# A gated MLP's feature tiles: ten instead of eight computed with seven block products for eight, and the block sums divided between VectorE and GpSimd

## The chip, the cores and the metric

One core of a Trainium2 chip runs the whole program. The metric is device time in microseconds (us) for one execution. Engines are named as the profile names them: PE is TensorE (matrix products), DVE is VectorE, ACT is ScalarE, POOL is GpSimd, and SP is SyncE, which here only issues DMAs. Each engine runs its own list of instructions in order and waits on semaphores.

## The reference, cut to what matters

The input x has 8 batches of 512 rows of 512 features. It is normalised to `xn`. One branch (a state-space layer) gives `s`, the other (a block with attention, a small modulation and a gated MLP) gives `g`, and the output is `x + s * g`. The change touches the gated MLP alone:

```
h = _rmsnorm(residual, ln2_w)                     # residual = xn, 512 features per row
gate_pre = h @ W_in_base.T + mod * (h @ A) @ B    # W_in_base: 2048 x 512, B: 16 x 2048
gate = silu(gate_pre)
up = h @ W_up_base.T                              # W_up_base: 2048 x 512
mlp_out = gate * up @ W_down.T                    # W_down: 512 x 2048
g = silu(residual + mlp_out)
out = x + s * g
```

`mod` is the modulation from the attention.

## The kernel before

The program computes the state-space branch first, then the attention (to about 1440 us of the span), then the MLP. The MLP is what the change touches, and it has two halves.

**Numbers in three products.** Each fp32 operand is split into a high part and its remainder; a product of two matrices is then high*high, high*low and low*high, so three matmuls stand for one (`project3`, lines 72 to 74). A high part comes from a copy into fp32r, the low part from a subtraction.

**First half.** The 2048 features of the MLP are 16 tiles of 128. Tiles 0 to 7 are computed in the plain way, batch by batch: step q = 8b + f is tile f of batch b, 64 steps in all. A step is, on PE, a "column" (gate: 4 pieces of the contraction by 3 matmuls and one for the modulation, line 2229; up: 12 matmuls) into the banks `PS[q % 2]` and `PS[2 + q % 2]`, and later a "down" (12 matmuls, lines 2253 to 2255) that adds into `PS[4..7]`. Between them stands the "product": ACT takes silu of the gate (`SG`, line 2279), DVE multiplies it with the up part (line 2302), ACT makes the high part `GH` (line 2282), DVE the low part `GL` (line 2304). PE's order is column q, down q - 1, column q + 1, down q: the product of step q has until PE has done down q - 1 and column q + 1. Steps 0 to 3 (EARLY) are done inside the attention. At the end of a batch DVE adds the skip `XT` to the four banks (`M`, line 2319) and SP stores them (`m_scratch`); in between DVE scales the skips (line 2309, four times).

**Second half.** Tiles 8 to 15 are taken as 4 units of 2 tiles, and the batches as 4 pairs. For a unit and a pair, the weights are a 2 x 2 block matrix (2 tiles by 2 halves of the contraction) and so are the rows (2 halves of the contraction by 2 batches). Their product is made with 7 block products for 8, from sums of blocks, for gate and for up. Step v (16 of them, `second_tensor`) is 14 block products of 6 matmuls, 4 modulation matmuls (line 2541) and 48 down matmuls (lines 2612 to 2614), 136 in all; ACT, DVE and POOL put the block products together (`U`, `P`, `G`, `HH`), and DVE adds the result to `MP` in SBUF (line 2704). After every pair (v = 4, 8, 12) silu, scaling by s and the skip finish the pair's 8 row tiles while the next pair runs. `SW` (7 sums of weights, two buffers), `DW2` and `XB` (7 blocks of rows) are loaded from scratch in DRAM.

**The jobs in between.** The sums of blocks must lie in DRAM when the second half begins. 36 jobs make them during the first half, all by POOL, through two buffers `JOB0` and `JOB1`: 16 "rows" jobs (7 instructions: add high and low, four sums of 256 columns, a cast and a subtraction to split 1024 columns), 16 "weights" jobs (8 instructions, a half of the contraction each, up to 896 columns wide) and 4 "outward" jobs (splitting a 1024-column piece of the down weights). `ffn_order` writes the order by hand: from q = 8 on, in two of three steps, the load of the next job, the job, and the store of its result. SP takes all loads and stores in this one order and waits, before each, for what it needs: a load for the last store from its buffer, a store for POOL.

**Passing over.** `second_ahead` (on SP) waits for the stores of all jobs and for 56 of 64 up parts, then loads `XB` 0 to 2, `SW` and `DW2` of the first unit, eight `MP` tiles, and after the last step the rest.

The names in the change: `GU` holds the split weights of the plain tiles, `DW` those of the down product, `FH`/`FL` the rows of a batch, `sw_scratch`, `dw_scratch` and `xt_scratch` the results of the jobs.

Of the kernel before, what the change touches and what calls it, by code (L numbers as in the profile page):

```python
# [19 lines left out]
HF = FF // 2  # L20
# [12 lines left out]
def build(nc, x, WinT, convw, convb, WxT, Alog, dtb, outWT, Dp, ln1, ln2, WqT, WkT, Wv, Wo, Aw, Bw, WgT, WuT, WdT,  # L33
          ident, umask, arow, maskt, maskT, out):
    ctx = ExitStack()
    with ctx:
# [2003 lines left out]
        GU.append(sb(re_, "GU1", [128, 4, 4, 512], F32R))  # L2040
# [3 lines left out]
        JOB = [sb(re_, "JOB0", [128, 2048], F32R)]  # L2044
        M1 = [sb(re_, f"M1{i}", [128, DM]) for i in range(4)]
        JOB.append(sb(re_, "JOB1", [128, 2048], F32R))
        re_.close()

# [15 lines left out]
        MP = [sb(hs, f"MP{i}", [128, DM]) for i in range(4)]  # L2064
        STR = [sb(hs, f"STR{i}", [128, DM]) for i in range(4)]
        MP += [sb(hs, f"MP{i}", [128, DM]) for i in range(4, 8)]
# [6 lines left out]
        sw_d = nc.dram_tensor("sw_scratch", [4, 128, 2, 2, 7, 2, 128], F32R, kind="Internal").ap()  # L2073
        dw_d = nc.dram_tensor("dw_scratch", [4, 128, 2, 2, DM], F32R, kind="Internal").ap()
# [792 lines left out]
```

## Time and profile before

| | us |
|---|---|
| median of 3 runs | 2478.18 |
| lowest and highest of them | 2475.45, 2478.62 |
| the profiled execution, its own time | 2479.31 |
| span of that execution's trace | 2477.3 |
| PE busy | 2400.3 (97%) |
| DVE busy | 1498.7 (60%) |
| ACT busy | 1108.8 (45%) |
| POOL busy | 708.8 (29%) |

The trace counts from the first to the last instruction; 2.0 us of the profiled execution's own time lie outside it. Matmuls are pipelined, so that one is shown as busy for longer than the distance to the next one; what a stretch of matmuls costs is read from their starts. An instruction of DVE or POOL that is held up by something other than a semaphore is shown as a longer instruction, not as idle time. In the page's chain of work that ended last PE has 80% and DVE 7%.

### The profile page before, as it was taken

How to read it: one execution, taken by the hardware profiler on the slowest of the kernel's cores; microseconds unless marked ns; L12 is line 12 of the kernel's file. 1: busy time of each engine (PE TensorE's matmuls, PEld its weight loads, DVE VectorE, ACT ScalarE, POOL GpSimd, SP SyncE). 2: the span in 40 equal slices, each digit the busy share in tenths (PEclk: the TensorE clock that was granted, in tenths of full speed). 3: DMA queues.
4: the chain of work that ended last, by engine and by line, in shares of the span. 5: the costliest groups of instructions: out<-in, count | busy, mean ns of one | idle time of the engine just before them, and what ended most of it. 6: DMA issues, size and time to landing. Idle time of an engine off the chain costs nothing.

```text
span 2477.3 us, 37647 instructions
## 1 busy us (share of the span) xinstructions
PE 2400.3 (97%) x13847; PEld 1944.4 (78%) x13847; DVE 1498.7 (60%) x3000; ACT 1108.8 (45%) x1895; POOL 708.8 (29%) x674
## 2 busy tenths in 40 slices
PE   7999999999999899999999999999999999999998
PEld 5878878778888777777777678888888887787876
DVE  7857667667565588888988853223332345454546
ACT  6444544544444377777777641111111233332333
POOL 4000000000001244454453616664647002121212
PEclk9999999999999999999999899999999999999999
DMA  4000100000003577676666426655555945555461
GB/s 146 18 35 1 35 18 18 35 18 18 17 1 107 184 208 215 201 201 192 178 182 201 129 77 208 217 198 188 194 199 175 351 174 205 203 189 219 163 245 68
DMA packets 190747, 348.65 MB, mean 141 GB/s; under 512 B 19008, under 2 KB 89664, under 8 KB 181840
## 3 DMA queue, kind: packets, MB, share of 16 engines
q1 hardware_dynamic: 188064, 345.91, 42.6%
q8 instruction: 112, 1.84, 0.3%
q10 hardware_dynamic: 2496, 0.29, 0.1%
q14 instruction: 75, 0.61, 0.1%
HBM read 234.70 MB, written 111.15 MB: 140 GB/s over the span
## 4 chain that ended last, share of the span: by engine, by line
PE 80%; DVE 7%; issue 5%; DMA 4%; ACT 2%; POOL 2%; SPq 1%; DVEq 0%; ACTq 0%; POOLq 0%
PE PS L72 12%; PE PS L74 12%; PE PS L73 12%; PE PS L1748 3%; PE PS L813 2%; PE PS L812 2%; PE PS L814 2%; PE PS L2253 2%; PE PS L2254 2%; PE PS L2255 2%; PE PS L1706 2%; PE PS L1725 2%; PE PS L1707 2%; PE PS L1708 2%; PE PS L2612 2%
## 5 line engine op out<-in xcount | busy, mean ns | idle before, releaser
L1912 DVE CUSTOM_DVE_ANT_0 PS<-PS,MK 128x512 f32<-128x512 f32 (+3 forms) x512 | 244.4, 503 | 70.5 <-PE PS L1725 68.7
L1848 ACT ACTIVATE PF<-PS 128x512 f32<-128x512 f32 (+1 forms) x384 | 201.0, 528 | 90.5 <-PE PS L1752 60.0
L2302 DVE TENSOR_TENSOR SG<-SG,PS 128x512 f32<-128x512 f32 x60 | 41.3, 688 | 290.9 <-PE PS L74 289.7
L72 PE MATMUL PS<-XH,WH 128*128 128x512 f32 x504 | 208.8, 414 | 0.0
L74 PE MATMUL PS<-XH,WL 128*128 128x512 f32 x504 | 197.6, 392 | 0.0
L73 PE MATMUL PS<-XL,WH 128*128 128x512 f32 x504 | 196.8, 390 | 0.0
L74 PE MATMUL PS<-FH,GU 128*128 128x512 f32 x480 | 187.9, 391 | 0.0
L73 PE MATMUL PS<-FL,GU 128*128 128x512 f32 x480 | 187.5, 391 | 0.0
L72 PE MATMUL PS<-FH,GU 128*128 128x512 f32 x480 | 187.4, 390 | 0.0
L1725 PE MATMUL PS<-KS,QS 96*128 96x512 f32 (+3 forms) x512 | 172.4, 352 | 13.2 <-DVE MX L1912 13.1
L72 PE MATMUL PS<-XB,SW 128*128 128x512 f32 x448 | 175.5, 392 | 4.4 <-ACT P L2669 3.6
L1917 DVE TENSOR_TENSOR PL<-PF,PH 128x1024 f16<-128x1024 f32 (+1 forms) x128 | 175.4, 1370 | 4.1 <-ACT PH L1853 4.1
L74 PE MATMUL PS<-XB,SW 128*128 128x512 f32 x448 | 175.3, 391 | 0.0
L73 PE MATMUL PS<-XB,SW 128*128 128x512 f32 x448 | 175.0, 391 | 0.0
L1748 PE MATMUL PS<-QS,KS 97*128 97x512 f32 (+3 forms) x512 | 170.1, 374 | 0.0
L1089 DVE SCALAR_TENSOR_TENSOR XC<-PS,CW,XC 128x511 f32<-128x511 f32 (+2 forms) x192 | 143.6, 748 | 33.6 <-ACT XC L950 28.6
L1853 ACT CAST PH<-PF 128x1280 f16<-128x1280 f32 x128 | 161.2, 1260 | 4.1
L2012 POOL TENSOR_TENSOR PL<-PF,PH 128x256 f16<-128x256 f32 x112 | 91.8, 819 | 190.9 <-ACT PH L1853 190.6
L2279 ACT ACTIVATE SG<-PS 128x512 f32<-128x512 f32 x60 | 36.0, 601 | 243.4 <-PE PS L2229 243.3
L2764 POOL TENSOR_TENSOR U<-U,P 128x512 f32<-128x512 f32 x16 | 20.8, 1297 | 386.5 <-ACT P L2669 386.5
L657 POOL TENSOR_TENSOR RSTD<-VT,MHALF 128x4 f32<-128x4 f32 x8 | 8.1, 1012 | 417.9 <-DVE VT L576 417.9
L1725 PEld LDWEIGHTS PS<-KS,QS 96*128 96x128 f32 x512 | 100.6, 203 | 27.1 <-DVE MX L1912 22.1
(352 smaller groups left out, 6644.5 us busy)
## 6 DMA issues: line engine op xcount, KB each, us to landing
SW<-sw_scratch SPq DMA_DIRECT2D x10, 3584.0 KB, 12.3
qk_scratch<-QT SPq DMA_DIRECT2D x128, 256.0 KB, 4.7
QS<-qk_scratch SPq DMA_DIRECT2D x96, 256.0 KB, 4.0
KS<-qk_scratch SPq DMA_DIRECT2D x96, 256.0 KB, 4.0
xt_scratch<-JOB SPq DMA_DIRECT2D x32, 512.0 KB, 3.5
XB<-xt_scratch SPq DMA_DIRECT2D x16, 1024.0 KB, 6.3
sw_scratch<-JOB SPq DMA_DIRECT2D x32, 448.0 KB, 3.3
DW<-dw_scratch SPq DMA_DIRECT2D x10, 1024.0 KB, 5.0
```

The lines of the kernel that those rows point to most:

```text
L72: pe.matmul(o, lh(k), xh(k), start=open_ and k == 0, stop=False, skip_group_check=True)
L73: pe.matmul(o, lh(k), xl(k), start=False, stop=False, skip_group_check=True)
L74: last = pe.matmul(o, ll(k), xh(k), start=False, stop=close and k == nk - 1, skip_group_check=True)
L812: pe.matmul(PS[bank][:, :], YH[u][:, c], OH[:, d, :], start=d == 0, stop=False, skip_group_check=True)
L1089: dve.scalar_tensor_tensor(out=y[:, j:], in0=p[:, 0:S - j], scalar=CW[:, d, 3 - j:4 - j], in1=y[:, j:], op0=ALU.mult, op1=ALU.add).then_in ...
L1725: t = pe.matmul(PS[2 + a % 2][:, at:at + n], QS[0:96, h, 128 * how:n], KS[0:96, h, 0:n], start=how != 1, stop=True, skip_group_check=True)
L1748: t = pe.matmul(p[:, at:at + n], KS[0:97, h, 128 * J:128 * J + 128], QS[0:97, h, 128 * J:512], start=len(how) == 2 and at == 0, stop=len(h ...
L1848: act.activation(PE_[u][:, o:o + at], PS[4 + a % 2][:, 0:at], ACT.Exp, scale=SC).then_inc(a_ex, 1)
L1853: act.copy(PH[u][:, :], PE_[u][:, :]).then_inc(a_ph, 1)
L1912: dve.tensor_tensor_reduce(out=p, in0=p, in1=MK[:, 512 - n:512], scale=1.0, scalar=NEG, op0=ALU.add, op1=ALU.max, accum_out=MX[w % 2][:, j ...
L1917: dve.tensor_tensor(PL[u][:, 0:n], PE_[u][:, 0:n], PH[u][:, 0:n], ALU.subtract).then_inc(a_rm, 1)
L2012: pool.tensor_tensor(PL[u][:, 1024:1280], PE_[u][:, 1024:1280], PH[u][:, 1024:1280], ALU.subtract).then_inc(a_rp, 1)
```

## The change

There are now 5 units of 2 tiles in the second half (tiles 6 to 15) and 6 plain tiles (`FIRST = 6`), so the first half has 48 steps and the second 20. The constants in waits follow. The two plain tiles' weights are not split in the first half any more (the slices 6 and 7 of `ffn_order`), and the skips are scaled at f = 4 instead of 6.

The jobs are laid out anew. The 16 rows jobs ("sums") are done by DVE, one in every second step from q = 8 to 38, behind that step's product and whatever else DVE has in it, through three buffers `JOBX`. POOL does 10 weights jobs, one in every fourth step, each now for the whole contraction (instructions twice as wide, up to 1792 columns) through a buffer `JOBW`, and 5 outward jobs through `JOBD`. SP has all of their loads and stores in one list.

In the second half, one modulation matmul goes to bank `DN[0]` instead of `ZG`; the first down product (t = 0) then waits for DVE's addition out of that bank, and t = 2 and 3 wait for earlier additions than before.

**DVE, first half, steps 6 to 9.** `SG` and `GL` are a step's product, `XT` the skips' scaling, `M` the end of a batch, `JOBX` a sums job. Before:

```order
L2302 TENSOR_TENSOR SG<-SG,PS 128x512
L2304 TENSOR_TENSOR GL<-SG,GH 128x512
L2309 TENSOR_SCALAR XT<-XT,MEAN,RSTD 128x512 x4
L2302 TENSOR_TENSOR SG<-SG,PS 128x512
L2304 TENSOR_TENSOR GL<-SG,GH 128x512
L2302 TENSOR_TENSOR SG<-SG,PS 128x512
L2304 TENSOR_TENSOR GL<-SG,GH 128x512
L2319 TENSOR_TENSOR M<-XT,PS 128x512 x4
```

The same engine in the changed kernel, the steps 9 and 10 with the job behind step 10:

```order
L2331 TENSOR_TENSOR SG<-SG,PS 128x512
L2333 TENSOR_TENSOR GL<-SG,GH 128x512
L2331 TENSOR_TENSOR SG<-SG,PS 128x512
L2333 TENSOR_TENSOR GL<-SG,GH 128x512
L2338 TENSOR_SCALAR XT<-XT,MEAN,RSTD 128x512 x4
L2420 TENSOR_TENSOR JOBX<-JOBX 128x1024
L2422 TENSOR_TENSOR JOBX<-JOBX 128x256
L2423 TENSOR_TENSOR JOBX<-JOBX 128x256
L2425 TENSOR_TENSOR JOBX<-JOBX 128x256
L2427 TENSOR_TENSOR JOBX<-JOBX 128x256
L2429 CAST JOBX<-JOBX 128x1024
L2431 TENSOR_TENSOR JOBX<-JOBX 128x1024
```

Seven instructions now stand between the product of an even step and that of the next.

**POOL, first half, its first work there.** Before, two rows jobs begin:

```order
L2385 TENSOR_TENSOR JOB<-JOB 128x1024
L2387 TENSOR_TENSOR JOB<-JOB 128x256
L2388 TENSOR_TENSOR JOB<-JOB 128x256
L2390 TENSOR_TENSOR JOB<-JOB 128x256
L2392 TENSOR_TENSOR JOB<-JOB 128x256
L2394 CAST JOB<-JOB 128x1024
L2396 TENSOR_TENSOR JOB<-JOB 128x1024
L2385 TENSOR_TENSOR JOB<-JOB 128x1024
```

Now a weights job (`JOBW`) and an outward job (`JOBD`):

```order
L2439 TENSOR_TENSOR JOBW<-JOBW,L2C 128x512
L2440 TENSOR_TENSOR JOBW<-JOBW,L2C 128x512
L2442 TENSOR_TENSOR JOBW<-JOBW 128x256
L2444 TENSOR_TENSOR JOBW<-JOBW 128x256
L2446 TENSOR_TENSOR JOBW<-JOBW 128x256
L2447 TENSOR_TENSOR JOBW<-JOBW 128x256
L2449 CAST JOBW<-JOBW 128x1792
L2451 TENSOR_TENSOR JOBW<-JOBW 128x1792
L2456 CAST JOBD<-JOBD 128x1024
L2458 TENSOR_TENSOR JOBD<-JOBD 128x1024
```

The rows jobs left POOL, and its longest instruction went from 1024 to 1792 columns.

**SP, the passage to the second half.** Before, the jobs' last stores and the loads of the second half:

```order
L2192 DMA XT<-in_x_dram 128x512 x4
L2355 DMA JOB<-in_WuT_dram 128x2x128 x2
L2374 DMA sw_scratch<-JOB 128x7x128
L2376 DMA sw_scratch<-JOB 128x7x128
L2359 DMA JOB<-in_WdT_dram 128x512 x2
L2374 DMA sw_scratch<-JOB 128x7x128
L2376 DMA sw_scratch<-JOB 128x7x128
L2374 DMA dw_scratch<-JOB 256x1x512
L2376 DMA dw_scratch<-JOB 256x1x512
L2449 DMA XB<-rh_scratch 128x1024
```

Now:

```order
L2381 DMA sw_scratch<-JOBW 128x1792 x2
L2235 DMA m_scratch<-M 128x512 x4
L2216 DMA XT<-in_x_dram 128x512 x4
L2374 DMA JOBW<-in_WuT_dram 128x512 x2
L2394 DMA dw_scratch<-JOBD 256x1x512 x2
L2381 DMA sw_scratch<-JOBW 128x1792 x2
L2490 DMA XB<-rh_scratch 128x1024
L2491 DMA XB<-rl_scratch 128x1024
L2494 DMA XB<-xt_scratch 128x2048 x2
L2477 DMA SW<-sw_scratch 128x7168
```

The load of the last weights job now stands behind the stores of a batch's four `M` tiles and the loads of the last skips.

The diff, cut to its core (the jobs' bodies keep their arithmetic):

```diff
-        PAIRS, UNITS = NB // 2, 4
+        PAIRS, UNITS, FIRST = NB // 2, 5, 6
...
+        WEIGHTS, OUTWARD, ROWS = 2 * UNITS, UNITS, 4 * PAIRS
...
-            yield "slice", 6
             yield "down", 3
-            ahead = 0
-            for q in range(EARLY + 1, 8 * NB):
-                b, f = divmod(q, 8)
+            for q in range(EARLY + 1, FIRST * NB):
+                b, f = divmod(q, FIRST)
...
-                if f == 6:
+                if f == FIRST - 2 or q == EARLY + 1:
                     yield "skips_scaled", b
-                if q == EARLY + 1:
-                    yield "slice", 7
-                if q >= 8 and q % 3 and ahead < len(jobs):
-                    if ahead == 0:
-                        yield "job", 0
-                    if ahead + 1 < len(jobs):
-                        yield "job", ahead + 1
-                    yield "job_kept", ahead
-                    ahead += 1
+                i = q - FIRST - 1
+                if i == -1:
+                    yield "weights_load", 0
+                    for n in range(3):
+                        yield "sums_load", n
+                if i < 0:
+                    continue
+                if i and i % 4 == 0 and i // 4 < WEIGHTS:
+                    yield "weights_load", i // 4
+                if i % 8 == 1 and i // 8 < OUTWARD:
+                    yield "outward_load", i // 8
+                if i >= 4 and i % 2 == 0 and i // 2 + 1 < ROWS:
+                    yield "sums_load", i // 2 + 1
+                if i % 4 == 0 and i // 4 < WEIGHTS:
+                    yield "weights_job", i // 4
+                if i % 8 == 2 and i // 8 < OUTWARD:
+                    yield "outward_job", i // 8
+                if i % 2 and i // 2 < ROWS:
+                    yield "sums_job", i // 2
+                if i % 4 == 2 and i // 4 < WEIGHTS:
+                    yield "weights_kept", i // 4
+                if i % 8 == 5 and i // 8 < OUTWARD:
+                    yield "outward_kept", i // 8
+                if i >= 3 and i % 2 and (i - 3) // 2 < ROWS:
+                    yield "sums_kept", (i - 3) // 2
...
-                sp.wait_ge(m_u, 60 if u == 0 else 8 * NB)
+                sp.wait_ge(m_u, FIRST * NB - 2 + 2 * u)
...
-            for r in range(2):
-                sp.wait_ge(j_st[r], j_st0[r] + 32 * len(range(r, len(jobs), 2)))
-            sp.wait_ge(m_u, 56)
+            sp.wait_ge(w_st, w_st0 + 32 * WEIGHTS)
+            sp.wait_ge(d_st, d_st0 + 32 * OUTWARD)
+            for r in range(3):
+                sp.wait_ge(x_st[r], x_st0[r] + 32 * len(range(r, ROWS, 3)))
+            sp.wait_ge(m_u, FIRST * NB - FIRST)
...
-                pe.wait_ge(n_ad, n_ad0 + 5 * v + 1)
-                modulate(pe, ZG, f1, b1, True).then_inc(n_pr, 1)
+                pe.wait_ge(*((n_ev, 8 * v - 3) if v else (m_fn, 4 * NB - 1)))
+                modulate(pe, DN[0], f1, b1, True).then_inc(n_pr, 1)
...
-                    if t < 2:
-                        pe.wait_ge(*((n_ev, 8 * v - 3 + t) if v else (m_fn, 4 * NB - 1 + t)))
+                    if t == 0:
+                        pe.wait_ge(n_ad, n_ad0 + 5 * v + 3)
+                    elif t == 1:
+                        pe.wait_ge(*((n_ev, 8 * v - 2) if v else (m_fn, 4 * NB)))
                     elif t < 4:
-                        pe.wait_ge(n_ad, n_ad0 + 5 * v + 5 - t)
+                        pe.wait_ge(n_ad, n_ad0 + 5 * v + t - 1)
...
-                dve.tensor_tensor(U3[0][:, :], U3[0][:, :], ZG[:, :], ALU.add).then_inc(n_ad, 1)
+                dve.tensor_tensor(U3[0][:, :], U3[0][:, :], DN[0][:, :], ALU.add).then_inc(n_ad, 1)
```

Here `m_u` counts up parts done, `n_ad` DVE's additions in the second half, `n_ev` the additions into `MP`.

## Rows read from the trace of the kernel before

**Rows 1.** The two largest waits of PE from 1440 us on: total, times, longest.

```profile
PE PS L2612 <- DVE HH L2743: 4.5, 3, 1.5
PE PS L72 <- ACT P L2669: 3.6, 3, 1.2
```

**Rows 2.** Busy time by stretch: PE, PEld, DVE, ACT, POOL, PE clock, DMA share, GB/s.

```profile
1500.00:1900.00 400.00, 400.00 (x1755) 329.60 (x1755) 129.26 (x142) 57.52 (x95) 245.47 (x230) 1.00 0.59 194
```

**Rows 3.** Timeline of DVE in two steps of the first half: start, duration.

```profile
1506.03 0.69 DVE L2302 TENSOR_TENSOR SG<-SG,PS 128x512 f32<-128x512 f32 x1 [6.38 <-PE PS L74]
1507.40 2.19 DVE L2304 TENSOR_TENSOR GL<-SG,GH 128x512 fp32r<-128x512 f32 x1 [0.69 <-ACT GH L2282]
...
1514.46 0.69 DVE L2302 TENSOR_TENSOR SG<-SG,PS 128x512 f32<-128x512 f32 x1 [4.88 <-PE PS L74]
1515.84 0.69 DVE L2304 TENSOR_TENSOR GL<-SG,GH 128x512 fp32r<-128x512 f32 x1 [0.69 <-ACT GH L2282]
```

**Rows 4.** Timeline of DVE in the second half: one instruction in two steps.

```profile
2031.97 0.69 DVE L2712 TENSOR_TENSOR G<-G,PS 128x512 f32<-128x512 f32 x1 [10.54 <-PE PS L74]
2062.98 0.69 DVE L2712 TENSOR_TENSOR G<-G,PS 128x512 f32<-128x512 f32 x1 [10.54 <-PE PS L74]
```

**Rows 5.** Timeline of POOL beside the first step of rows 3.

```profile
1506.64 2.40 POOL L2385 TENSOR_TENSOR JOB<-JOB 128x1024 f32<-128x1024 f32 x1 [62.85 <-DMA JOB<-rl_scratch]
1509.12 1.07 POOL L2387 TENSOR_TENSOR JOB<-JOB 128x256 f32<-128x256 f32 x1
```

**Rows 6.** Groups by line, first half: count, busy us, mean ns, idle before.

```profile
L2304 DVE TENSOR_TENSOR GL<-SG,GH 128x512 fp32r<-128x512 f32 x60 | 64.7, 1078 | 41.2 <-ACT GH L2282 41.2
```

**Rows 7.** Views of single DVE lines: duration ns min/median/max, first and last start.

```profile
L1205 DVE TENSOR_TENSOR EX<-EX,DTB x8: 1221/1224/1226, 63.6 to 754.0; 128x1024 f32<-128x1024 f32 x8
L1221 DVE TENSOR_TENSOR PFM<-MD,MASK x16: 418/422/426, 68.5 to 759.3; 128x256 f32<-128x256 f32 x16
L2309 DVE TENSOR_SCALAR XT<-XT,MEAN,RSTD x32: 534/831/2653, 1474.2 to 1948.3; 128x512 f32<-128x512 f32 x32
L2319 DVE TENSOR_TENSOR M<-XT,PS x32: 678/681/689, 1491.8 to 1960.5; 128x512 f32<-128x512 f32 x32
```

**Rows 8.** The same of POOL lines, by tile.

```profile
L1985 POOL TENSOR_TENSOR STGC<-STGC,L2C x8: 1034/1266/2286, 1365.4 to 1402.3; 128x512 f32<-128x512 f32 x8
L2387 POOL TENSOR_TENSOR JOB<-JOB x16: 736/744/1097, 1509.1 to 1868.9; 128x256 f32<-128x256 f32 x16
L2394 POOL CAST JOB<-JOB x16: 1039/1041/1406, 1512.5 to 1872.2; 128x1024 fp32r<-128x1024 f32 x16
L673 POOL TENSOR_TENSOR WL<-ZS,WH x1: 4694/4694/4694, 19.4 to 19.4; 128x2048 fp32r<-128x2048 f32 x1
```

**Rows 9.** DMA landing times: issues by line from 1500 to 1900, then `SW` at 1920 to 1930.

```profile
xt_scratch<-JOB SPq DMA_DIRECT2D x32, 512.0 KB, 3.5
JOB<-in_WdT_dram SPq DMA_DIRECT2D x6, 256.0 KB, 2.9
DMA to landing us min/median/max: 17.8/17.8/17.8
```

**Rows 10.** Timeline of SP and PE at the passage to the second half.

```profile
1925.70 0.58 SPq L2436 DMA_DIRECT2D SW<-sw_scratch  x1
...
1958.52 0.39 PE L72 MATMUL PS<-XB,SW 128*128 128x512 f32 x1
```

**Rows 11.** Timeline of PE and DVE: a plain step, then the pair's change (v = 4).

```profile
2038.70 0.68 DVE L2728 TENSOR_TENSOR U<-U,PS 128x512 f32<-128x512 f32 x1
2040.67 0.39 PE L2612 MATMUL PS<-DW,HH 128*128 128x512 f32 x1
2104.83 0.39 PE L2612 MATMUL PS<-DW,HH 128*128 128x512 f32 x1
2106.02 0.69 DVE L2728 TENSOR_TENSOR U<-U,PS 128x512 f32<-128x512 f32 x1 [2.50 <-POOL U L2764]
2111.93 0.50 PE L2612 MATMUL PS<-DW,HH 128*128 128x512 f32 x1 [1.50 <-DVE HH L2743]
```

More of the change, by code:

```diff
@@ L2310, in ffn_vector @@
                                           ALU.subtract, ALU.mult).then_inc(m_xn, 1)
-                elif kind == "down" and q % 8 == 7:
-                    h = q // 8
+                elif kind == "sums_job":
+                    sum_rows(dve, q)
+                elif kind == "down" and q % FIRST == FIRST - 1:
+                    h = q // FIRST
                     dve.wait_ge(m_dn, q + 1)
@@ L2325, in ffn_pool, with load_weights @@
                     attn_pool(pool, [("inverse", n, None)])
-                elif kind == "job":
-                    do_job(pool, n)
+                elif kind == "weights_job":
+                    sum_weights(pool, n)
+                elif kind == "outward_job":
+                    split_outward(pool, n)
             second_pool(pool)
-        def job_loads(n):
-            return sum(64 if jobs[i][0] == "rows" else 32 for i in range(n % 2, n + 1, 2))
-        def job_ops(n):
-            return sum({"rows": 7, "weights": 8, "outward": 2}[jobs[i][0]] for i in range(n + 1))
-        def load_job(sp, n):
-            kind, a, j, k = jobs[n]
-            J = f32(JOB[n % 2][:, :])
-            if n >= 2:
-                sp.wait_ge(j_st[n % 2], j_st0[n % 2] + 32 * (n // 2))
+        def load_weights(sp, n):
+            u, j = divmod(n, 2)
+            J = f32(JOBW[:, :])
+            if n:
+                sp.wait_ge(w_st, w_st0 + 32 * n)
             else:
@@ new lines, in load_outward, with keep_outward @@
+        def load_outward(sp, n):
+            J = f32(JOBD[:, :])
+            if n:
+                sp.wait_ge(d_st, d_st0 + 32 * n)
+            for f in range(2):
+                sp.dma_start(J[:, 512 * f:512 * f + 512], wd_[FIRST + 2 * n + f]).then_inc(d_ld, 16)
+        def keep_outward(sp, n):
+            J = f32(JOBD[:, :])
+            for x, c in ((0, 1024), (1, 0)):
+                sp.wait_ge(d_op, d_op0 + 2 * n + 1 + x)
+                sp.dma_start(f32(dw_d[n])[:, :, x, :], J[:, c:c + 1024].rearrange("p (f m) -> p f m", f=2)).then_inc(d_st, 16)
@@ new lines, in load_sums @@
+        def load_sums(sp, n):
+            p, k, t = n // 4, n // 2 % 2, n % 2
+            J = f32(JOBX[n % 3][:, :])
+            if n >= 3:
+                sp.wait_ge(x_st[n % 3], x_st0[n % 3] + 32 * (n // 3))
+            for x, rows in enumerate((rh_d, rl_d)):
+                for b in range(2):
+                    c = 1024 * x + 512 * b
+                    sp.dma_start(J[:, c:c + 512].rearrange("p (k t) -> p k t", k=2),
+                                 f32(rows[2 * p + b])[:, k::2, 256 * t:256 * t + 256]).then_inc(x_ld[n % 3], 16)
@@ L2438, in load_unit @@
             if free is None:
[L2439 removed]
+                sp.wait_ge(m_dn, FIRST * NB - 4 + 2 * u)
             else:
@@ L2760, in second_pool @@
                 if v and v % UNITS == 0:
-                    for n in range(2 * v - 8, 2 * v):
+                    for n in range(8 * (v // UNITS) - 8, 8 * (v // UNITS)):
                         skipped(n)
```

234 lines of the change are left out of this document (118 added, 116 removed).

## The prediction

> **What bounds the kernel now.** I read the waits of PE first, then the busy time by stretch, then DVE's and POOL's timelines. In the MLP PE waits for next to nothing: its two largest waits, 4.5 and 3.6 us, are three each, at the changes of a pair in the second half [rows 1]. In the first half PE is busy for 400.00 of 400.00 us at the full granted clock (1.00), while POOL is busy for 245 and DVE for 129 [rows 2]. So PE's own work sets the time here, and an edit pays only as far as PE gets less to do and the others go on keeping up. One step of the first half takes 1514.46 - 1506.03 = 8.43 us [rows 3], that is 37 matmuls at 0.228. One step of the second half takes 2062.98 - 2031.97 = 31.01 us [rows 4], 136 matmuls at 0.228. Both are bare PE time.
>
> **What is removed and added on PE.** 16 plain steps go: 16 x 8.43 = 134.9 us. 4 steps of the second half come: 4 x 31.01 = 124.0 us. Net -10.9 us, the price of 592 - 544 = 48 matmuls. The two split weights of tiles 6 and 7 (on ACT and DVE) go too; PE never waited for them, so they are worth nothing. A unit's added load of `SW` lies under a 31 us step, like the ten there are now; so do the added steps' DVE, ACT and POOL work. These go at zero.
>
> **The change of a pair.** The new wait of the first down product is for DVE's addition L2728. In a plain step that ends at 2038.70 + 0.68 = 2039.38, and the down products begin at 2040.67 [rows 11]: 1.3 us to spare, nothing lost. At a pair's change they begin at 2104.83, but the addition ends at 2106.71: the first four down tiles come 1.9 us later. But PE then stops anyway at the fifth, until 2111.93, for the low part of the last hidden tile [rows 11]. Four tiles take 24 x 0.228 = 5.5 us, so the fifth could start at 2112.2: the new wait eats the old one and costs 0.3 us. Three changes: +0.9 us (0 to 1.5).
>
> **The sums on DVE.** A sums job is two additions of 1024 columns, four of 256 and a cast of 1024: 2 x 1.22 + 4 x 0.42 [rows 7] plus the cast. The trace has no such cast on DVE; between 0.53 (a scaling of half the columns) and 1.22 (an addition as wide) I take 0.8, nearer to the one-input row. Waits between dependent instructions and the overlap of others about cancel: 5.2 us (4.9 to 5.7). 16 jobs add 83 us to an engine that is idle for two thirds, and lie beside PE. What counts is the delay of the next product. Let T be the end of the column of an even step. The product's multiplication starts 0.2 later, and the low part `GL` ends 2.1 us after that start (1514.46 to 1516.53 [rows 3]), at T + 2.3. The job follows; at f = 4 the four scalings (2.1 us alone [rows 7]) stand ahead of it, at f = 0 the four additions `M` (0.68 each, from T + 2.9). So the job ends at T + 7.5, T + 9.6 or T + 10.8. Down of the next step needs its `GL` two steps after T, at T + 16.9, and that takes 2.1 us: the job may end at T + 14.8. The slack is 7.3, 5.2 or 4.0 us. Undisturbed, the jobs cost PE nothing.
>
> **Where they are disturbed.** `GL` has two inputs in SBUF. When it meets an instruction of POOL it gets longer: it lasts 2.19 us where POOL's runs from 1506.64 to 1509.04, and ends at 1509.59, 0.55 after it; then POOL's next lasts 1.07 instead of 0.74 [rows 3, 5, 8]. The multiplication out of PSUM stays at 0.69. So the two engines take turns, whole instructions at a time, which makes `GL` 1078 ns long on average [rows 6] instead of 690 [rows 3]. All seven instructions of a sums job are of DVE's kind that can be held, the additions surely, the cast probably. The Trainium skill says so too (SBUF — State Buffer, Who interferes with whom): a DVE instruction with both inputs in SBUF and a GpSimd instruction that reads SBUF exclude each other for the whole instruction. The trace agrees (ends 0.55 us behind POOL's). By the same section the scalings and the cast hold the pair as well, if they run in their two-port mode; 831 ns median against 534 alone [rows 7] fits that.
>
> A weights job on POOL is now 2 x 1.03 (512 columns, scaled) + 4 x 0.74 + a cast of 1792 (1.04 for 1024 [rows 8], estimate 1.7) + a subtraction of 1792 (between 2.40 for 1024 [rows 5] and 4.69 for 2048: estimate 4.1), 10.8 us, with small gaps 11.2. With five outward jobs of 3.5, POOL works 130 of the 346 us of 41 steps, 37% against 61% before. If a weights job begins beside a sums job, the two alternate: DVE's 5.2 us get 4 to 6.7 longer by POOL's first six or seven instructions, and the next `GL` can meet the 4.1 us subtraction. For step 16 (f = 4) I laid the rows end to end with the weights job beginning at T + 3.8: the sums job ends at T + 13.5 instead of T + 9.6, the multiplication and the copy at T + 14.9, the subtraction holds `GL` until T + 17.3, it ends at T + 17.9, and PE waits 1.0 us. That is one such place. Laid out in this way over 41 steps, SP's list included, the jobs drift against each other, and with every duration moved between its bounds three or four places lose 0.3 to 5 us each; the rest stay within the slack. I take +5.5 us in all (0 to 10).
>
> **The passage.** Let T be the end of column 42. The second half can begin at T + 5 x 8.43 + 5.5 = T + 47.6. SP must store the four `M` of batch 6 (the last is added at T + 5.4) and load four skips, some 8 us after T, before it loads the last weights job: landing 2.9 [rows 9], POOL 11.2, the store's landing 3.5 for 512 KB [rows 9], up to 6 for the 896 KB here. Then four loads of blocks, and `SW` goes out at T + 29 to T + 31. The first `SW` landed 17.8 us after its issue [rows 9], issued at 1925.70 for use at 1958.52 [rows 10]: it had 15 us to spare. Now it lands at T + 47 to T + 49: 0 to 1.4 us late, 4 if the queue of transfers is longer than before. I take +1.0.
>
> **The sum.** -10.9 + 0.9 + 5.5 + 1.0 = -3.5 us. The profiled execution took 2479.31 us, 1.1 above the median 2478.18. 2479.3 - 3.5 = 2475.8, as a median 2474.7.
>
> **The rivals.** First, the slack suffices (-10.9 + 0.9 + 0 to 2 = -9): 2469.2. For it: before, POOL was busy for 61% of the time and PE did not wait once for `GL`. Against it: DVE had then one instruction to be held in a step, now up to twelve.
>
> Second, slower: the turns between DVE and POOL lock in. SP's list ties the load of a weights job to the store of a sums job two behind, so the same phase can come back at every fourth step. If the subtraction of 4.1 us meets a sums job or its `GL` in eight places at 2 us each, that is +16 us instead of 5.5, the total +7.0: 2485.2. It decides from the point where a job ends later than T + 14.8. The general advice of the Trainium skill (Perfetto Trace Analysis, Optimizing Scalar/DVE Operations) is that shifting work between these two may not help, since they share the port; here it would make this rival.
>
> Third, slower: transfers. 194 GB/s for 400 us, 77.6 MB, kept the DMA engines at 0.59 [rows 2]; now some 92 MB of the first half go into 350 us, a share near 0.8, and every load in SP's list waits for an earlier store to land. Sums loads have three buffers and land four steps ahead, 34 us, but if five jobs wait 3 us beyond the slack, +15 us: 2490.
>
> Fourth, the gain is not there since a second-half step gets longer: 20 steps by 0.5 us would take 10 us: 2484.7. Only a wait that eats the 1.3 us of rows 11 does that.
>
> **Chances.** Forecast 0.45, its own range 2470.5 to 2479; slack suffices 0.25; lock-in 0.17; transfers 0.08; longer steps 0.05. Faster by over 0.2% (5 us, about what a measurement of this kernel can tell from no change) is below 2473.2: all of the first rival and a quarter of the forecast, 0.36. Slower by as much is above 2483.1: lock-in for the most part and the last two, 0.20. Within: 0.44. The range is 2467.5 to 2484.
>
> **What would show it.** PE's waits in the first half, now absent: for DVE's `GL` in three or four places, some 5 us in all. DVE's 1024-column additions at 1.22 us alone and longer beside POOL; POOL's subtraction near 4.1. At the three pair changes, a wait for the addition of about 2 us and none or little at the fifth down tile. One wait of 0 to 2 us for `SW` ahead of the second half. Steps of 8.43 and 31.01 us unchanged between waits. I am wrong if a sums job waits for its load, or if PE stops at other places than these.

## The result and the profile after

The changed kernel takes 2486.83 us (median of 22 runs, 2471.26 to 2495.52) where the kernel before, beside it, takes 2479.48 (22 runs). The ratio is 1.0026, with a 95% interval of 1.0015 to 1.0036: slower by 0.26%, where I had forecast 3.5 us less. On another chip the same kernel gave 1.0023 (1.0010 to 1.0036). The profiled execution took 2485.09 us with a span of 2483.2, against 2479.31 and 2477.3.

The waits of PE from 1360 us on, which answer to [rows 1], with total, times and longest (waits inside the attention are left out):

```profile
PE PS L2284 <- DVE GL L2333: 7.4, 3, 4.0
PE PS L2657 <- DVE U L2773: 5.4, 3, 1.9
PE PS L72 <- ACT P L2714: 2.7, 3, 1.2
PE PS L72 <- DMA XB<-xt_scratch: 1.9, 1, 1.9
PE PS L72 <- ACT P L2720: 0.8, 3, 0.3
PE PS L72 <- DMA SW<-sw_scratch: 0.5, 1, 0.5
PE PS L72 <- DMA XB<-rl_scratch: 0.5, 1, 0.5
```

The first line is new: the first down product of a step waits for the low part `GL`, three times. The three DMA lines are new too: the passage. The busy time by stretch of the first half, as in [rows 2]:

```profile
1500.00:1830.00 330.00, 322.60 (x1393) 264.36 (x1392) 189.45 (x236) 46.10 (x76) 126.50 (x83) 0.98 0.76 269
```

PE is no longer busy for all of it, and its clock is 0.98 on average, not 1.00. DVE went from 129 of 400 us to 189 of 330, POOL from 245 to 127, and the DMA share to 0.76. The second half's step is what it was, as in [rows 4]:

```profile
2039.74 0.69 DVE L2757 TENSOR_TENSOR G<-G,PS 128x512 f32<-128x512 f32 x1 [10.54 <-PE PS L74]
2070.75 0.69 DVE L2757 TENSOR_TENSOR G<-G,PS 128x512 f32<-128x512 f32 x1 [10.54 <-PE PS L74]
```

**The worst of the three places.** DVE's timeline at steps 16 and 17 (start, duration; column 16 ended at 1556.6, 0.2 ahead of its `SG`):

```profile
1562.08 1.76 DVE L2420 TENSOR_TENSOR JOBX<-JOBX 128x1024 f32<-128x1024 f32 x1
...
1566.52 1.79 DVE L2427 TENSOR_TENSOR JOBX<-JOBX 128x256 f32<-128x256 f32 x1
1568.34 4.43 DVE L2429 CAST JOBX<-JOBX 128x1024 fp32r<-128x1024 f32 x1
1572.80 1.94 DVE L2431 TENSOR_TENSOR JOBX<-JOBX 128x1024 fp32r<-128x1024 f32 x1
1574.67 0.68 DVE L2331 TENSOR_TENSOR SG<-SG,PS 128x512 f32<-128x512 f32 x1
1576.02 1.47 DVE L2333 TENSOR_TENSOR GL<-SG,GH 128x512 fp32r<-128x512 f32 x1 [0.68 <-ACT GH L2311]
```

POOL's timeline beside it:

```profile
1566.27 1.76 POOL L2449 CAST JOBW<-JOBW 128x1792 fp32r<-128x1792 f32 x1
1568.11 4.11 POOL L2451 TENSOR_TENSOR JOBW<-JOBW 128x1792 fp32r<-128x1792 f32 x1
1572.16 1.50 POOL L2456 CAST JOBD<-JOBD 128x1024 fp32r<-128x1024 f32 x1
```

And PE's:

```profile
1573.20 0.39 PE L74 MATMUL PS<-FH,GU 128*128 128x512 f32 x1
1577.55 0.79 PE L2284 MATMUL PS<-DW,GH 128*128 128x512 f32 x1 [3.96 <-DVE GL L2333]
1578.14 0.63 PE L2285 MATMUL PS<-DW,GH 128*128 128x512 f32 x1
1578.57 0.63 PE L2286 MATMUL PS<-DW,GL 128*128 128x512 f32 x1
```

The addition L2427 takes 1.79 us instead of 0.42 and ends 0.28 after POOL's cast. POOL's subtraction of 1792 columns has begun by then, at 1568.11, and DVE's cast comes behind it, at 1568.34. The cast, 0.69 alone, lasts 4.43 and ends at 1572.77, 0.55 after the subtraction. POOL's next cast and DVE's last subtraction (1.94 us instead of 1.23) do the same once more. The two engines take turns, one instruction each. So the sums job ends at 1574.74 and PE stands for 4.1 us. The view of the single line over all 16 jobs:

```profile
L2429 DVE CAST JOBX<-JOBX x16: 693/695/4429, 1496.5 to 1758.5; 128x1024 fp32r<-128x1024 f32 x16
```

**PE comes back slow.** Three stretches of PE in the changed kernel, with PE's busy time and, as the last three numbers, its clock, the DMA share and GB/s: right behind the wait of 4.1 us, behind the one at 1681 to 1684, and during a wait at a pair's change, in which the clock is at 1.00.

```profile
1577.55:1582.50 4.95, 4.95 (x12) 0.50 0.70 295
1685.40:1688.60 3.20, 3.20 (x9) 0.50 0.77 323
2015.10:2017.33 2.23, 0.40 (x3) 1.00 0.58 166
```

At a granted clock of 0.50, the level of 1.2 GHz, matmuls follow each other by 0.43 us and not by 0.228. Twelve of them after the first wait cost 2.4 us more, eight after the other 1.7.

### The profile page after: what moved, and what is told of

The parts are those of the page before. It is cut to its first block, busy times and chain, and to the rows that moved or that the text cites. A ratio compares the mean times of both kernels' runs of the same rounds, so it can differ in the third digit from the quotient of the medians.

```text
span 2483.2 us, 37643 instructions
## 1 busy us (share of the span) xinstructions
PE 2393.6 (96%) x13799; PEld 1936.1 (78%) x13799; DVE 1608.5 (65%) x3154; ACT 1124.1 (45%) x1921; POOL 597.5 (24%) x524
## 4 chain that ended last, share of the span: by engine, by line
PE 74%; DVE 9%; issue 5%; DMA 5%; POOL 2%; ACT 2%; SPq 2%; DVEq 0%; ACTq 0%; POOLq 0%
PE PS L72 11%; PE PS L74 11%; PE PS L73 11%; PE PS L813 2%; PE PS L812 2%; PE PS L814 2%; PE PS L1748 2%; PE PS L2657 2%; PE PS L2658 2%; PE PS L2659 2%; PE PS L1706 2%; PE PS L1725 2%; PE PS L1707 2%; PE PS L1708 2%; PE PS L798 1%
## 5 line engine op out<-in xcount | busy, mean ns | idle before, releaser
L72 PE MATMUL PS<-XB,SW 128*128 128x512 f32 x560 | 219.6, 392 | 6.4 <-ACT P L2714 2.7
L74 PE MATMUL PS<-XB,SW 128*128 128x512 f32 x560 | 219.1, 391 | 0.0
L73 PE MATMUL PS<-XB,SW 128*128 128x512 f32 x560 | 218.7, 391 | 0.0
L2749 DVE TENSOR_TENSOR MP<-MP,PS 128x512 f32<-128x512 f32 x160 | 107.8, 685 | 60.3 <-PE PS L2659 60.3
L2809 POOL TENSOR_TENSOR U<-U,P 128x512 f32<-128x512 f32 x20 | 26.3, 1316 | 489.8 <-ACT P L2714 489.8
L74 PE MATMUL PS<-FH,GU 128*128 128x512 f32 x352 | 137.8, 391 | 0.0
L72 PE MATMUL PS<-FH,GU 128*128 128x512 f32 x352 | 137.7, 391 | 0.0
L73 PE MATMUL PS<-FL,GU 128*128 128x512 f32 x352 | 137.6, 391 | 0.0
L72 PEld LDWEIGHTS PS<-XB,SW 128*128 128x128 f32 x560 | 105.3, 188 | 32.7 <-issue 3.9
L2757 DVE TENSOR_TENSOR G<-G,PS 128x512 f32<-128x512 f32 x20 | 13.7, 687 | 180.5 <-PE PS L74 180.5
L2657 PE MATMUL PS<-DW,HH 128*128 128x512 f32 x320 | 125.3, 392 | 5.4 <-DVE U L2773 5.4
```

What stands on the lines that cost most here:

```text
L72: pe.matmul(o, lh(k), xh(k), start=open_ and k == 0, stop=False, skip_group_check=True)
L73: pe.matmul(o, lh(k), xl(k), start=False, stop=False, skip_group_check=True)
L74: last = pe.matmul(o, ll(k), xh(k), start=False, stop=close and k == nk - 1, skip_group_check=True)
L2657: pe.matmul(bank[:, :], high, DW2[u % 2][:, f, 0, :], start=f == 0, stop=False, skip_group_check=True)
L2749: dve.tensor_tensor(MP[i][:, :], MP[i][:, :], DN[i % 4][:, :], ALU.add).then_inc(n_ev, 1)
```

## The experiments

Theory A: PE waits because DVE's job meets POOL's long instructions, which hold single instructions of a dependent chain; the slow clock behind a wait adds half as much again. Theory B: DVE's queue alone is too full. Theory C: loads come late, through SP's list. The ratios are to the kernel before, on the same chip.

**pool_idle and dve_idle.** One engine's jobs are cut to a few columns, the other's stay.

```diff
-            pool.tensor_tensor(R_[:, 0:1792], J[:, 0:1792], J[:, 2048:3840], ALU.subtract).then_inc(w_op, 1)
+            pool.tensor_copy(R_[:, 0:4], J[:, 2048:2052]).then_inc(w_op, 1)
```

In pool_idle POOL's other instructions are cut likewise, in dve_idle those of `sum_rows`:

```diff
-            dve.tensor_copy(R_[:, 0:1024], J[:, 1024:2048]).then_inc(x_op, 1)
+            for i in range(6):
+                dve.tensor_copy(R_[:, 0:4], J[:, 1024:1028]).then_inc(x_op, 1)
+                dve.wait_ge(x_op, done + i + 1)
```

> The changed kernel with POOL's weights and outward jobs cut to a few columns per instruction; loads, stores, waits and the sums jobs on DVE stay. What is left out: the sums of the weights and the splitting of the down weights, so the units' weights are not the right ones. Theory A (DVE and POOL take turns, and PE halves its clock after a long wait): no wait of PE for GL in the first half; against the kernel before -10.9 us (steps), +1.3 (pairs), 0 to +2 at the passage, since the last weights job is over 11 us earlier: about -8.5 us, ratio 0.9965. Theory B (the sums jobs are too long for DVE's queue by themselves): the waits for GL stay, ratio 1.000 or more. Theory C (transfers and SP's list): the same waits as in the changed kernel, ratio 1.002.

> The changed kernel with the sums jobs on DVE cut to a few columns per instruction; POOL's jobs, all loads, stores and waits stay. What is left out: the sums of the rows. Theory A: POOL's instructions can hold GL for 4.1 us at most, the slack is 6.1: no wait for GL, the passage as in the changed kernel (+3.5 us): -10.9 + 1.3 + 3.5 = -6 us, ratio 0.9975. Theory B: the same. Theory C: waits of PE stay, ratio 1.002.

Measured: 0.9955 (0.994 to 0.997) and 0.9976 (0.9966 to 0.9986). In neither does PE wait for `GL`. From 1440 us on, all of PE's waits of pool_idle, but for one of 0.7 in the attention, are at the pair changes:

```profile
PE PS L72 <- ACT P L2713: 4.4, 3, 2.2
PE PS L2656 <- DVE U L2772: 4.1, 3, 1.7
...
PE PS L72 <- ACT P L2719: 0.5, 2, 0.2
```

B falls: in pool_idle DVE has all its work. C falls for these waits: in dve_idle SP's list and all transfers are whole, the passage still costs 4.3 us (1.2 for `SW`, 3.1 for a block), and nothing waits for `GL`. With no wait but those at the pair changes the change is worth 0.45% or 11 us (7 to 15), beside the -10.9 of the sum.

**split_pool and sub_in_pieces.** POOL's cast of 1792 columns in 4 pieces, its subtraction in 7, those of 1024 in 2 and 4; then the subtraction of 1792 alone:

```diff
-            pool.tensor_tensor(R_[:, 0:1792], J[:, 0:1792], J[:, 2048:3840], ALU.subtract).then_inc(w_op, 1)
+            for c in range(0, 1792, 256):
+                t = pool.tensor_tensor(R_[:, c:c + 256], J[:, c:c + 256], J[:, 2048 + c:2304 + c], ALU.subtract)
+            t.then_inc(w_op, 1)
```

> The changed kernel, whole, with POOL's cast of 1792 columns in four pieces and its subtraction in seven of 256 (outward jobs alike). A piece lasts at most 0.74 us instead of 4.1. Theory A: each turn costs DVE 0.8 us at most, a sums job beside POOL takes about 10 us; waits for GL go from 7.4 us to 2 or less and no half clock follows: 7 to 9 us faster than the changed kernel, ratio 0.9990 to 0.9995 against before. A rival of A: more turns are taken, the sum of POOL's work beside a job is what counts, and the waits stay as they are: 1.002.

> The changed kernel with one instruction cut: POOL's subtraction of 1792 columns becomes seven of 256; its cast of 1792 (1.7 us) and the outward instructions stay whole. Theory A (the 4.1 us subtraction holds the cast of a sums job and GL): the cast lasts at most about 2.5 us and the waits for GL go, 11 us less than the changed kernel: ratio 0.9982 (0.9972 to 0.999), close to split_pool's 0.9976. Rival (any turns cost the same, since the pieces alternate with DVE's just as well and POOL's job only gets longer): waits for GL remain, ratio above 1.001.

Measured: 0.9976 (0.9966 to 0.9985) and 0.9985 (0.9971 to 1.0000). Both do all of the work. The same place in split_pool, DVE and then POOL:

```profile
1566.56 0.93 DVE L2429 CAST JOBX<-JOBX 128x1024 fp32r<-128x1024 f32 x1
1567.52 1.46 DVE L2431 TENSOR_TENSOR JOBX<-JOBX 128x1024 fp32r<-128x1024 f32 x1
...
1570.27 1.01 DVE L2333 TENSOR_TENSOR GL<-SG,GH 128x512 fp32r<-128x512 f32 x1 [0.69 <-ACT GH L2311]
```

```profile
1566.31 3.61 POOL L2450 CAST JOBW<-JOBW 128x448 fp32r<-128x448 f32 x4
1570.00 5.36 POOL L2454 TENSOR_TENSOR JOBW<-JOBW 128x256 fp32r<-128x256 f32 x7
```

DVE's cast lasts 0.93 instead of 4.43, and `GL` is ready 6.2 us earlier (1571.28 against 1577.49). POOL pays, 5.36 us for its subtraction instead of 4.11, and has the time. No wait for `GL` is left in split_pool, one of 0.4 us in sub_in_pieces: the one long instruction is the cause of nearly all of it.

**held_steps.** The kernel before, with DVE held ahead of `GL` in ten steps by sums over `DW` into a spare tile, so that PE waits for chosen times.

```diff
+                    if q in held:
+                        for i in range(2):
+                            dve.tensor_reduce(JUNK[:, 2 * at + i:2 * at + i + 1], ..., AX.X, ALU.add)
                     dve.tensor_tensor(GL[g][:, :], SG[u][:, :], f32(GH[g][:, :]), ALU.subtract).then_inc(m_gl, 1)
```

> The kernel before with DVE held ahead of GL in ten plain steps, by two reductions of the down weights into spare columns, so that PE waits for about 1.0, 1.5, 2.0, 2.5, 3.0, 3.5, 4.0, 5.0, 7.0 and 9.0 us. Its output is the reference's. If the clock falls after a long wait, the matmuls behind the longer ones start 0.43 us apart instead of 0.227 for some time, as behind two waits of the changed kernel (4.0 and 2.5 us); behind the shortest they do not. If it does not depend on the wait, all ten read alike. Sum of the waits 38 us, plus some 2.4 us for each that halves the clock.

Measured, in one run: 2528.01 us, 48.7 above the profiled execution of before, of which the waits are 37.2. PE's waits, and then three stretches of PE with clock, DMA share and GB/s last:

```profile
PE PS L2254 <- DVE GL L2311: 37.2, 10, 8.5
```

```profile
1605.37:1607.57 2.20, 2.20 (x10) 1.00 0.84 268
1735.72:1737.92 2.20, 2.20 (x5) 0.50 0.87 257
1878.75:1880.95 2.20, 2.20 (x5) 0.50 0.41 129
```

The stretches stand right behind pauses of PE's issue of 2.49, 4.38 and 7.14 us. Of the ten pauses, the five of 3.48 to 8.93 us were all followed by 8 to 13 matmuls at 0.43; of the others (1.70, 2.00, 2.49, 2.66, 2.99) only that of 2.66 was, by 8. 60 matmuls at 0.20 us more each make 12 us, near the 11.5 by which the time grew more than the waits.

**odd_steps.** The sums jobs one step later, where neither `XT` nor `M` stands ahead of them.

```diff
-                if i % 2 and i // 2 < ROWS:
-                    yield "sums_job", i // 2
+                if i >= 2 and i % 2 == 0 and i // 2 - 1 < ROWS:
+                    yield "sums_job", i // 2 - 1
```

(loads and stores move with them.)

> The changed kernel with its long POOL instructions whole; the 16 sums jobs stand in the steps of odd number (f = 1, 3, 5), one step later than now, so that neither the four scalings nor the four additions M stand ahead of one. Theory A (a held-up sums job is late only where its slack of 5.2 or 4.0 us is short): with 7.3 us everywhere, the two or three waits of PE for GL (7.4 us in all and 4 us more at half clock) go or fall to one of under 1 us; ratio to the kernel before 0.9985 (0.997 to 1.000). Theory D (what matters is only how often a subtraction of 4.1 us meets a sums job, the slack being small beside it): three or more waits of 2 us or more remain, ratio 1.002 to 1.004.

Measured: 1.0006 (0.9993 to 1.0018), between the two theories. The waits for `GL` shrink to 2.0, but one of 2.6 for `M` comes, behind this `GL`:

```profile
1580.26 4.96 DVE L2431 TENSOR_TENSOR JOBX<-JOBX 128x1024 fp32r<-128x1024 f32 x1
...
1586.51 2.61 DVE L2333 TENSOR_TENSOR GL<-SG,GH 128x512 fp32r<-128x512 f32 x1 [0.69 <-ACT GH L2311]
1589.04 2.47 DVE L2350 TENSOR_TENSOR M<-XT,PS 128x512 f32<-128x512 f32 x4
```

More slack takes part of the loss away, not all: what stood ahead of the job now stands behind it, and POOL's long instructions hold whatever they meet. Here the weights job's subtraction (4.38 us) holds the end of the sums job, and the outward job's (2.37) holds `GL`.

**sub_after_sums.** All instructions whole; POOL's subtraction waits for the sums job beside it.

```diff
+            if 2 * n < ROWS:
+                pool.wait_ge(x_op, x_op0 + 7 * (2 * n + 1))
             pool.tensor_tensor(R_[:, 0:1792], J[:, 0:1792], J[:, 2048:3840], ALU.subtract).then_inc(w_op, 1)
```

> The changed kernel, all instructions whole, with one wait added: POOL's subtraction of 1792 columns waits until the sums job that runs beside its weights job is done. Nothing gets shorter, POOL's jobs only end later. Theory A (the loss comes where that subtraction holds the cast of a sums job, so that the job ends too late): no cast of a sums job lasts more than about 2.5 us, the waits of PE for GL (7.4 us) and the half clock behind them (4 us) go but for one of at most 1 us where the subtraction meets GL itself; ratio to the kernel before 0.998 (0.9968 to 0.9992), if the passage gets no later. Rival (any work of POOL's beside DVE costs, wherever it is put: the subtraction now holds GL instead): waits for GL of 5 us or more in all remain, ratio 1.001 or more.

Measured: 0.9993 (0.9979 to 1.0008). At step 16 on DVE:

```profile
1566.11 2.05 DVE L2429 CAST JOBX<-JOBX 128x1024 fp32r<-128x1024 f32 x1
1570.71 3.45 DVE L2333 TENSOR_TENSOR GL<-SG,GH 128x512 fp32r<-128x512 f32 x1 [0.69 <-ACT GH L2311]
```

The cast is let go and 4.6 of 7.4 us of waiting are gone, but the subtraction starts at 1569.57, right behind the job, and then holds `GL`: two waits, 2.8 us in all, where I had given at most one, of 1 us.

**sums_on_pool.** The sums jobs on POOL, in the same order and spaces.

```diff
-                elif kind == "sums_job":
-                    sum_rows(dve, q)
...
+                elif kind == "sums_job":
+                    sum_rows(pool, n)
```

> The changed kernel with the 16 sums jobs done by POOL instead of DVE, in the same spaces and at the same place in the order. POOL then has some 16 x 9 + 10 x 11.2 + 5 x 3.5 = 270 us of work in 41 steps (346 us), DVE only its products. Theory A (a held-up DVE costs time only since its jobs are a chain of seven instructions ahead of the next product): no wait of PE for GL; the first half costs nothing beyond its steps; ratio to the kernel before 0.9975 (0.996 to 0.999), the rest being the passage, where the last weights job may end up to 5 us later. Rival 1 (POOL falls behind: sums and weights jobs in one line of 30 of 34 us in four steps, with SP waiting for each): the passage waits 10 us or more for SW, ratio 1.001 or more. Rival 2 (the share of time in which POOL is busy is what hurts DVE): waits for GL of over 5 us.

Measured: 0.9985 (0.9975 to 0.9995), no wait for `GL`, though POOL is busy for 84% of the first half and `GL` is held more than in any other kernel (mean 1294 ns; 891 in the changed kernel, 1130 in the one before). The first half by stretch, with the columns of [rows 2], and then the group of `GL` with those of [rows 6], from 1440 to 1830 us:

```profile
1500.00:1820.00 320.00, 320.00 (x1404) 263.70 (x1403) 128.21 (x128) 46.43 (x76) 269.76 (x195) 1.00 0.79 280
```

```profile
L2333 DVE TENSOR_TENSOR GL<-SG,GH 128x512 fp32r<-128x512 f32 x44 | 56.9, 1294 | 30.2 <-ACT GH L2311 30.2
```

So neither POOL's load nor the holding as such costs time, but the held chain of seven instructions on the way to the next product does. The Trainium skill (Perfetto Trace Analysis, Optimizing Scalar/DVE Operations) says that work shifted between the two engines may bring nothing; here it brought 0.4% the one way.

**The passage: early_load, last_load.** Both have POOL's instructions in pieces. In early_load every load of a weights job stands one step earlier in SP's list, in last_load only the last one:

```diff
+                if q == FIRST * NB - FIRST:
+                    yield "weights_load", WEIGHTS - 1
                 yield "column", q
```

and in early_load:

```diff
+                if i > 0 and i % 4 == 3 and (i + 1) // 4 < WEIGHTS:
+                    yield "weights_load", (i + 1) // 4
                 yield "column", q
```

> The changed kernel with POOL's long instructions in pieces (as in split_pool), and in addition each load of a weights job one step earlier in SP's list, so that the last one stands ahead of the stores of a batch's four M and of the last skips, not behind them. Theory (SP's list makes SW late): split_pool still waited 2.3 us for SW and 0.3 us for a block at the passage; the last weights job's load is issued some 6 us earlier or more, so the two waits go: 2.6 us less than split_pool, ratio to the kernel before 0.9965 (0.9955 to 0.9975), and no wait of PE for GL. Rival (SW is late since the transfers ahead of it are long, whatever the order): the wait for SW stays at 2 to 3 us and the ratio at 0.9976. Second rival: the load waits for the last job's stores at a worse place, SP falls behind with the rows or skips, and PE waits there for them by over 2 us: 0.998 or more.

> The changed kernel with POOL's long instructions in pieces, and one load moved: that of the last weights job stands one step earlier in SP's list, ahead of a batch's M stores. All other loads stay (early_load moved all nine, and SP, which waits for the last job's stores before each, fell behind step by step, so that job 8 began 13 us later than in split_pool). Theory (the chain load, POOL's job, store, SW sets the passage): in split_pool the load was issued at 1783.38 and the stores of the job before were issued by 1771.6, so the load can go out about 6 us earlier, the job ends 6 us earlier, SW lands ahead of its use: the wait of 2.3 us and the matmuls at half clock behind it (1.6 us) go. Ratio to the kernel before 0.9962 (0.9952 to 0.9974). Rival (the transfers bound the passage, 434 GB/s at a DMA share of 1.05 from SW's issue on): SW goes out earlier but PE waits as long, 0.9976 or more.

Measured: 0.9996 (0.9985 to 1.0007) and 0.9964 (0.9949 to 0.9978). When SP issues the last job's load and the first `SW`, in early_load and then the latter in last_load:

```profile
1787.53 0.81 SPq L2374 DMA_DIRECT2D JOBW<-in_WuT_dram  x2
1809.36 0.70 SPq L2485 DMA_DIRECT2D SW<-sw_scratch  x1
```

```profile
1803.62 0.32 SPq L2487 DMA_DIRECT2D SW<-sw_scratch  x1
```

In split_pool the two were issued at 1783.38 and 1807.90. Moving all loads made the last one later, not earlier: SP waits before each for the job before to be stored, and every other load and store behind it moves back. The load of the ninth of ten jobs went out at 1767.8, where split_pool had 1753.6. PE then waited 3.9 us for `SW`. Moving one brought `SW` out 4.3 us earlier, and PE waits for nothing at the passage.

**bank_undone and last_load_bank.** The modulation matmul back in `ZG`, with the waits of before; on split_pool and on last_load.

```diff
-                pe.wait_ge(*((n_ev, 8 * v - 3) if v else (m_fn, 4 * NB - 1)))
-                modulate(pe, DN[0], f1, b1, True).then_inc(n_pr, 1)
+                pe.wait_ge(n_ad, n_ad0 + 5 * v + 1)
+                modulate(pe, ZG, f1, b1, True).then_inc(n_pr, 1)
```

> The changed kernel with POOL's long instructions in pieces, and in the second half the modulation matmul back in bank ZG with the waits of the kernel before. Theory (the new wait of the first down product costs some 0.3 to 0.5 us at each of three pair changes and nothing else): PE's waits at the pair changes are then those of before, 4.5 for the last hidden tile and 3.6 for P, and the time is 0.9 us less than split_pool, ratio 0.9972 (0.9966 to 0.9978). Rival (the bank change gained something within the plain steps): the time is more than split_pool's 0.9976 by 0.0004 or more, and a plain step is longer than 31.01 us. Nothing here changes the first half: no wait for GL.

> last_load (POOL's long instructions in pieces, the last weights job's load one step earlier) and in addition the modulation matmul back in bank ZG with the waits of the kernel before. Theory (the new wait of the first down product costs 0.3 us at each of three pair changes, 0.9 us): PE's waits at the changes fall from 5.3 + 3.4 + 0.7 us to 4.0 to 4.5 + 2.6 to 3.6 + 0.8; time 0.9 us less than last_load on the same chip, ratio to the kernel before 0.9961 where last_load has 0.9964. Rival (the old place is worse, since its own wait for the last hidden tile is 1.7 us and the half clock can follow it as well): 0.5 us or more above last_load.

> last_load once more, beside last_load_bank and the changed kernel on one chip. Expected ratio to the kernel before 0.9964 (0.9952 to 0.9976), no wait of PE for GL, SW or a block.

Measured: 0.9979 (0.9967 to 0.9990) where split_pool had 0.9976 on another chip; and on one chip 0.9957 (0.9943 to 0.9972) against 0.9955 (0.9942 to 0.9968) for last_load. The wait of 5.2 for `U` becomes one of 4.0 for `HH`; that for `P` is 3.3 beside 2.0, but last_load's other execution had 3.4. The bank change costs nothing that can be measured: the intervals are some 3 us either way, so neither forecast is borne out or refuted. last_load, at 0.9955 to 0.9964, beats both kernels and does all of the work.

**changed_again.** The changed kernel a second time.

> The changed kernel itself on the chip of the two above, to see whether its waits come at the same places in another execution. Theory A: waits of PE for GL in the steps 9, 17 and 29 again, 6 to 9 us in all, and one or more stretches at half clock; ratio to the kernel before 1.0026 (1.0012 to 1.004), so last_load is 15 us below it. Rival (the places are chance, since DVE and POOL drift against each other): other steps, between one and five of them.

Measured: 1.0023 (1.0010 to 1.0036). The waits for `GL` are at the same three steps:

```profile
PE PS L2284 <- DVE GL L2333: 8.2, 3, 4.0
```

So they come with the order of the jobs and are not chance. At step 28 the phase was another, though. DVE, then POOL's subtraction:

```profile
1675.27 1.79 DVE L2422 TENSOR_TENSOR JOBX<-JOBX 128x256 f32<-128x256 f32 x1
1676.98 4.28 DVE L2423 TENSOR_TENSOR JOBX<-JOBX 128x256 f32<-128x256 f32 x1
```

```profile
1676.86 4.11 POOL L2451 TENSOR_TENSOR JOBW<-JOBW 128x1792 fp32r<-128x1792 f32 x1
```

Here an addition of 256 columns has the 4.28 us, and it does not depend on the one ahead of it. PE's wait is the same, 2.4 us for 2.5: here it made no difference which link of the chain was held.

## Why the prediction was wrong, point by point

**PE's own work, -10.9 us: right.** The steps are 8.44 and 31.01 us, and pool_idle, in which little else is left, gives 11 us (7 to 15). The durations that I had estimated held too: the cast of a sums job 0.69 us (0.8, [rows 7]), POOL's cast of 1792 columns 1.76 (1.7) and its subtraction 4.11 (4.1, [rows 5, 8]).

**The pair changes, +0.9: right in kind, too small to tell.** `U` takes the place of the fifth down tile's wait, as said (5.4 for 4.5). By the steps of DVE's L2757 the three changes took 1.2 us more than in the profile of before. But 1.6 us of it are slow clock, eight matmuls at 0.43 behind the pause of 2.25 us at the second change, so that the waits themselves are no longer than before. The timed runs find no difference.

**The turns of DVE and POOL, +5.5 (0 to 10): the step that failed.** Its places, three, and its cause were right, its price was 12.0: pauses longer than in a running stream by 1.2 (step 9), 4.1 (17) and 2.6 us (29), 7.9 in all, and 4.1 us of slow clock. The pauses alone lie inside the 0 to 10.

The larger error is the clock. A wait of PE was priced at its own length; the matmuls at 0.43 us behind it were in none of my terms, put at nothing without a reason. Before, no wait in the MLP was over 1.5 us [rows 1] and none showed it.

The smaller one, 2.4 us, is in the length of the waits, and shows in the worked example of step 16. The turns were as I had them, one instruction each. Over the two executions of the changed kernel I find 81 instructions of sums jobs and `GL` that were held (over 0.06 us longer than alone), and none by more than one of POOL's. What was off is where the two lists met. With T = 1556.6 the weights job began at T + 3.0 and not at T + 3.8. Its first instructions held the scalings (3.36 us for four, not 2.1), so the sums job began at T + 5.5, not T + 4.4. The subtraction ran from T + 11.5, not T + 13.2, and so met the cast, a link of the chain, and not `GL`. Behind it the outward job, which the example does not name, held the last subtraction and then `GL` (1.47). The cast lasted 4.43 us, the job ended at T + 18.1 and not T + 13.5, and PE waited 4.0 us, not 1.0. The same cast lasts 4.42 and 4.43 us at steps 8 and 28, the two other places. The rule that I had (the Trainium skill, SBUF — State Buffer, Who interferes with whom: the two exclude each other for a whole instruction) held. A held instruction that takes 0.69 us alone ended 0.53 to 0.56 us behind POOL's end, an addition of 256 columns 0.27 to 0.29.

**The passage, +1.0 (0 to 1.4, up to 4): mis-sized, 3.4.** `SW` was issued at 1817.66, inside what I gave, landed 17.8 us later as in [rows 9], and cost 0.5 us of waiting as a term of 0 to 1.4 allows. What I left out is what stands behind it in SP's list:

```profile
1817.66 0.64 SPq L2477 DMA_DIRECT2D SW<-sw_scratch  x1
1818.35 0.65 SPq L2483 DMA_DIRECT2D DW<-dw_scratch  x1
1819.04 14.01 SPq L2502 DMA_DIRECT2D MP<-m_scratch  x8
1833.10 1.85 SPq L2494 DMA_DIRECT2D XB<-xt_scratch  x1
...
1845.88 0.50 PE L72 MATMUL PS<-XB,SW 128*128 128x512 f32 x1 [1.95 <-DMA XB<-xt_scratch]
```

The eight `MP` loads keep SP for 14 us while the DMA engines are full (436 GB/s, a share of 1.05, from 1820 to 1830). Block 3 went out at 1833.10, 2.4 us ahead of the second half's first matmul, and landed 12.7 us later; before, it had gone out 5.2 us ahead. A list that is late is late for all that stands in it, not for its first entry alone.

**The sum.** -10.9 + 1.2 + 12.0 + 3.4 = +5.7; the span grew by 5.9. The forecast was 9.2 us below that sum: 4.1 for the slow clock behind the waits for `GL`, 2.4 for those waits, 2.4 for the passage and 0.3 for the pair changes. Of the rivals, lock-in had the right time (2485.2) and half of the mechanism: the phase does come back, beside the weights jobs 0, 2 and 5, but in these three places and not in eight. Transfers were not it: the sums jobs waited for a load once, 0.4 us (1.3 in the second execution). The range stopped at 2484.0 since the turns were cut at 10 us, and lock-in at 0.17 lay outside it. 1.3 us of the distance are the kernel before itself, 2479.48 here and 2478.18 where the forecast began.

## What to carry to other kernels

Where two engines take turns, each link of a chain can meet one instruction of the other. So price the chain with the longest one at any link, and not only at the place where one layout puts it. Cutting that instruction up helps: here seven pieces for one turned 1.0026 into 0.9976 to 0.9985, and cost POOL 1.3 us a job. A pause of TensorE can cost more than its length, here up to 2.6 us more. To spare a list of loads one late entry, move that entry alone.

## What the runs showed of the hardware that I had not expected

- With work in both lists DVE and POOL take turns one for one. At step 16 POOL's subtraction begins 0.08 us after its cast ends, while DVE's held addition still runs, and so is ahead of DVE's next: a cast of 0.69 us took 4.43, an addition of 0.42 took 4.28.
- The clock at half (granted 0.50, 1.2 GHz) followed each of the pauses of PE's issue of 3.48 to 8.93 us in held_steps, for 8 to 13 matmuls, at a cost of 1.6 to 2.6 us. It also followed some shorter ones (2.25 at a pair's change of the changed kernel, 2.71 at the passage of split_pool). It did not follow one of 3.57 us in sub_in_pieces, and of the same pause at step 29 it followed that of 2.84 us in the first execution and not that of 2.82 in the second. What decides it is open.
- A cast of 1024 columns to fp32r takes DVE 0.69 us, and a subtraction of 1792 on POOL 4.05 to 4.11 us as one, 5.36 as seven beside DVE.
